# Second attention: three key blocks of a pass exponentiated on VectorE, value runs of two blocks, six sets of results

## What is computed

```python
q = (x @ wq + bq).reshape(B, Sq, H, D).transpose(0, 2, 1, 3)     # 16 heads of 8, Sq = 1024
k = (y @ wk + bk).reshape(B, -1, H, D).transpose(0, 2, 1, 3)     # 6404 keys
v = (y @ wv + bv).reshape(B, -1, H, D).transpose(0, 2, 1, 3)
scores = jnp.einsum('bhqd,bhkd->bhqk', q, k) / jnp.sqrt(D)
attn = jax.nn.softmax(scores, axis=-1)
out = jnp.einsum('bhqk,bhkd->bhqd', attn, v)
```

## Time and profile before

| what | value |
|---|---|
| median of 3 runs | 1854.99 us |
| profiled execution, its own time | 1853.31 us |
| its span, first to last instruction | 1851.5 us |
| mean granted TensorE clock | 0.924 of full speed |
| PE busy | 1582.9 us (85% of the span) |
| ACT busy | 1373.1 us (74%) |
| DVE busy | 854.8 us (46%) |
| POOL busy | 169.9 us (9%) |

### The profile page before, as it was taken

One profiled execution on the slowest core, in us unless ns is written; L12 is line 12 of the kernel. 1 busy time (PEld: TensorE's weight loads), 2 busy tenths in 40 slices (PEclk: granted clock), 3 DMA queues, 4 the chain that ended last, 5 costly groups with the idle time before them and its releaser, 6 DMA issues. The chain is left out here.

```text
span 1851.5 us, 22757 instructions
## 1 busy us (share of the span) xinstructions
PE 1582.9 (85%) x8261; PEld 603.4 (33%) x8261; DVE 854.8 (46%) x2331; ACT 1373.1 (74%) x1441; POOL 169.9 (9%) x154
## 2 busy tenths in 40 slices
PE   6789788898998993776789999999999999985996
PEld 4463354554554552533211111111111111113442
DVE  7768999999999997473400000000000000003223
ACT  5737687888887874313289999999999999982332
POOL 4840211111111101000000000000000000000000
PEclk8869899999999996787689999999999999997998
DMA  3430968979769679350000004000500000003000
GB/s 103 144 117 0 184 150 177 202 155 210 174 151 230 152 179 241 78 152 7 18 1 1 1 1 63 13 1 1 75 1 1 1 1 1 1 1 98 0 1 12
DMA packets 69263, 143.41 MB, mean 77 GB/s; under 512 B 21993, under 2 KB 40642, under 8 KB 68218
## 3 DMA queue, kind: packets, MB, share of 16 engines
q0 software_dynamic: 13616, 75.73, 20.5%
q1 hardware_dynamic: 55098, 65.30, 13.2%
q10 hardware_dynamic: 432, 0.85, 0.1%
HBM read 52.65 MB, written 13.99 MB: 36 GB/s over the span
## 5 line engine op out<-in xcount | busy, mean ns | idle before, releaser
L1936 ACT ACTIVATE ex<-ps 128x1536 f32<-128x1536 f32 x536 | 721.9, 1494 | 6.0 <-PE ps L1890 6.0
L1905 PE MATMUL ps<-ex,V 128*9 128x512 f32 x3200 | 419.8, 597 | 0.5 <-ACT ex L1936 0.4
L850 PE MATMUL ps<-K,qst 128*128 128x512 f32 (+1 forms) x832 | 392.9, 604 | 30.7 <-ACT srow L920 20.7
L1890 PE MATMUL ps<-Q,K 52*128 52x512 bf16 (+1 forms) x1632 | 322.8, 385 | 39.1 <-ACT ex L1936 34.2
L1946 DVE COPY o<-ps 9x512 f32<-9x512 f32 x32 | 22.0, 687 | 714.2 <-PE ps L1909 713.5
L1051 DVE MAX8 cand<-srow 128x8 f32<-128x200 f32 (+1 forms) x1024 | 318.7, 359 | 8.7 <-ACT srow L920 8.6
L1011 DVE SCALAR_TENSOR_TENSOR both<-srow,top,both 128x1536 f32<-128x1536 f32 (+1 forms) x128 | 239.4, 1870 | 21.2 <-ACT both L937 21.0
L920 ACT COPY srow<-ps 128x1024 f32<-128x1024 f32 (+1 forms) x224 | 205.1, 924 | 46.1 <-PE ps L850 45.7
L937 ACT ACTIVATE both<-srow,shift 128x1536 f32<-128x1536 f32 (+1 forms) x128 | 209.4, 1638 | 23.2 <-DMA both<-both 21.8
L1890 PEld LDWEIGHTS ps<-Q,K 52*128 52x128 bf16 (+1 forms) x1632 | 60.7, 94 | 448.1 <-ACT ex L1936 433.1
L850 PEld LDWEIGHTS ps<-K,qst 128*128 128x128 f32 x832 | 150.8, 198 | 166.5 <-issue 116.1
(11 more groups left out here) (333 smaller groups left out, 1087.2 us busy)
## 6 DMA issues: line engine op xcount, KB each, us to landing
both<-both POOLq DMA_DIRECT2D x69, 768.0 KB, 8.9
v_ring<-v_rows SPq DMA_DIRECT2D x84, 256.0 KB, 6.3
both<-both POOLq DMA_DIRECT2D x23, 898.0 KB, 13.1
K<-k_parts SPq DMA_DIRECT2D x48, 204.0 KB
k_parts<-kl SPq DMA_DIRECT2D x12, 384.0 KB, 2.6
V<-v_rows SPq DMA_DIRECT2D x4, 900.0 KB, 6.7
v_rows<-v1g SPq DMA_DIRECT2D x12, 288.0 KB, 3.8
srow<-v_rows SPq DMA_DIRECT2D x1, 3200.0 KB, 17.5
```

The source lines that it names most:

```text
L850: last = M.matmul(ps[:, BANK_OF[item] + b, 0:c1 - c0], qst[:, h, :], K0[:, c0:c1], start=True, stop=True)
L1890: last = M.matmul(out, K1[rows_, quad % 2, hh // 2, keys], Q1[rows_, 4 * quad + hh, tb * TB:(tb + 1) * TB], start=True, stop=True, tile_po ...
L1905: last = M.matmul(out, V1[:, quad % 2, g, VW * j:VW * j + VW], ex1[:, slot(w, 4 * g + j), :], start=g == 0, stop=False, tile_position=(0, ...
L1936: C.activation(ex1[:, s:s + NBANK, :], ps[:, b:b + NBANK, :], ACT.Exp)\
```

## The change

- **Scores in powers of two.** The queries' scale is multiplied by log2(e), and ScalarE's exponential takes scale = ln 2 and a bias. The bias is a tile of one value per partition, `common`, filled by POOL behind the clearing of `o1`; ScalarE waits for it once (`common_ready`).
- **Three key blocks per pass on VectorE.** Key blocks 47, 48 and 49 (12 tiles) no longer go through ScalarE. In units 6, 11, 16, ... 61 (`OWN`) ScalarE has only two tiles, and the third bank of the unit holds one of these 12 tiles. VectorE computes 2^x for it with nine dependent instructions of 512 elements (`power_of_two`): a maximum out of PSUM, an addition that rounds, six `scalar_tensor_tensor` and an integer shift. PE's scores wait for VectorE's reading of that bank too (`own_read`). ScalarE's part is 47 blocks and the last tile, 189 tiles, still in 67 units.
- **Values of two blocks in one run.** Key blocks 2i and 2i+1 are summed together behind the unit at which the second is ready. The values of VectorE's blocks follow behind units 26, 46 and 66 (`own_values`).
- **Six sets of results.** `ex1` has 18 slots (six units), `power` eight.

```diff
-        SC1 = float(DH1) ** -0.5
+        SC1 = float(DH1) ** -0.5 * LOG2E
...
-        NSLOT, NBANK = 12, 3
-        ex1 = sb(b8, "ex1", [P, NSLOT, TB])
+        NBANK, NHELD = 3, 6
+        BATCH, BATCHES, EVERY, FIRST_U = 4, 3, 5, 6
+        NOWN = BATCH * BATCHES
+        OWN = [FIRST_U + EVERY * i for i in range(NOWN)]
+        REGULAR = FULL1 - BATCHES
...
+        LATE_AT = {OWN[BATCH * (b + 1) - 1] + EVERY: b for b in range(BATCHES)}
+        LAST_OF = [min(4 * g + 3, NTILE - 1) for g in range(NSUM)]
+        READY_AT = [PLACE[tile][0] + 2 for tile in LAST_OF]
+        READY_AT = [READY_AT[min(g | 1, NSUM - 2)] if g < NSUM - 1 else READY_AT[g] for g in range(NSUM)]
...
                 PL.memset(o1[:, :, :], 0.0).then_inc(S("o1_zero"), 1)
+                PL.memset(common[:, :], float(np.log(1.0 / LEAD))).then_inc(S("common_ready"), 1)
...
                     if w * NU + u >= 2:
                         pe.wait_ge(S("exped1"), w * NU + u - 1)
+                        if own_before(w * NU + u - 1):
+                            pe.wait_ge(S("own_read"), own_before(w * NU + u - 1))
...
+                    if u in OWN:
+                        b, j = divmod(OWN.index(u), BATCH)
+                        last = score_tile(w, ps[:, bank(w, u, NBANK - 1), :], 0, REGULAR + b, j)
                     last.then_inc(S("scored1"), 1)
...
+                def own_values(w, b):
+
+                    quad = w // NB
+                    pe.wait_ge(S("powered"), w * NOWN + BATCH * (b + 1))
+                    for j in range(BATCH):
+                        last = M.matmul(ps[32 * j:32 * j + VW, 6 + w % 2, :], V1[:, quad % 2, REGULAR + b, VW * j:VW * j + VW],
+                                        power[:, (w * NOWN + BATCH * b + j) % (2 * BATCH), :], start=False, stop=False,
+                                        tile_position=(0, 32 * j))
+                    last.then_inc(S("power_used"), 1)
...
+                        if u in LATE_AT:
+                            own_values(w, LATE_AT[u])
...
+                act.wait_ge(S("common_ready"), 1)
...
-                        C.activation(ex1[:, s:s + NBANK, :], ps[:, b:b + NBANK, :], ACT.Exp)\
+                        C.activation(ex1[:, s:s + n, :], ps[:, b:b + n, :], ACT.Exp, scale=LN2, bias=common[:, 0:1])\
                             .then_inc(S("exped1"), 1)
...
+                def power_of_two(w, i):
+
+                    m = w * NOWN + i
+                    if m:
+                        dve.wait_ge(S("powered"), m)
+                    dve.wait_ge(S("scored1"), w * NU + OWN[i] + 1)
+                    V.tensor_scalar(score[:, :], ps[:, bank(w, OWN[i], NBANK - 1), :], LOW2, None, ALU.max)\
+                        .then_inc(S("own_read"), 1)
+                    dve.wait_ge(S("own_read"), m + 1)
+                    dchain(V.tensor_scalar(whole_[:, :], score[:, :], ROUND2, None, ALU.add))
+                    dchain(V.scalar_tensor_tensor(part[:, :], whole_[:, :], ROUND2, score[:, :], ALU.subtract, ALU.subtract))
+                    dchain(V.scalar_tensor_tensor(poly[:, :], part[:, :], POWER[4], part[:, :], ALU.add, ALU.mult))
+                    for k in (3, 2, 1):
+                        dchain(V.scalar_tensor_tensor(poly[:, :], poly[:, :], POWER[k], part[:, :], ALU.add, ALU.mult))
+                    bits = whole_[:, :].bitcast(I32)
+                    dchain(V.tensor_scalar(bits, bits, 23, None, ALU.logical_shift_left))
+                    if m // BATCH >= 2:
+                        dve.wait_ge(S("power_used"), m // BATCH - 1)
+                    V.scalar_tensor_tensor(power[:, m % (2 * BATCH), :], poly[:, :], POWER[0], whole_[:, :], ALU.add, ALU.mult)\
+                        .then_inc(S("powered"), 1)
```

More of the change, by code:

```diff
@@ L42 @@
 LOWEST = -3.0e38
-EXP_RANGE = 60.0
+LOG2E = float(np.log2(np.e))
+LN2 = float(np.log(2.0))
+EXP_RANGE = 60.0 * LOG2E
 LN_EPS = 1e-5
@@ L1853, in bank @@
[L1853 to L1857, removed]
+        NBANK, NHELD = 3, 6
[3 more added lines that the diff above has]
+        REGULAR = FULL1 - BATCHES
+        NPASS = NQ * NB
+        NTILE = 4 * REGULAR + 1
+        NSUM = REGULAR + 1
+        ex1 = sb(b8, "ex1", [P, NHELD * NBANK, TB])
+        power = sb(b8, "power", [P, 2 * BATCH, TB])
@@ new lines, in program @@
+        score, whole_, part = (sb(b8, name, [P, TB]) for name in ("score", "whole_part", "part"))
+        poly = score
+        common = sb(b8, "common", [P, 1])
+        UNITS, at = [], 0
+        while at < NTILE:
+            n = NBANK - 1 if len(UNITS) in OWN else NBANK
+            UNITS.append(list(range(at, at + n)))
+            at += n
+        NU = len(UNITS)
+        assert at == NTILE and max(OWN) + EVERY < NU
+        PLACE = {tile: (u, n) for u, tiles in enumerate(UNITS) for n, tile in enumerate(tiles)}
@@ L1859, in program, with block_of, own_before, bank @@
+        def block_of(g):
+            return g if g < REGULAR else FULL1
+        def own_before(k):
+            w, u = divmod(k, NU)
+            return w * NOWN + sum(1 for o in OWN if o < u)
+        def bank(w, u, n):
+            return (w * NU + u) % 2 * NBANK + n
+        def slot(w, u, n):
+            return (w * NU + u) % NHELD * NBANK + n
         with nc.Block() as block:
@@ L1873, in _, with score_tile @@
             def _(pe):
+                def score_tile(w, out, col, g, hh):
+                    quad, tb = divmod(w, NB)
+                    rows_ = slice(64 * (hh % 2), 64 * (hh % 2) + ROWS1)
+                    keys = slice(g * P, (g + 1) * P) if g < FULL1 else slice(g * P, g * P + LEFT)
+                    return M.matmul(out, K1[rows_, quad % 2, hh // 2, keys], Q1[rows_, 4 * quad + hh, tb * TB:(tb + 1) * TB],
+                                    start=True, stop=True, tile_position=(64 * (hh % 2), col))
                 def scores(w, u):
@@ L1879, in scores @@
                         pe.wait_ge(S("exped1"), w * NU + u - 1)
[L1880 to L1892, removed]
+                        if own_before(w * NU + u - 1):
+                            pe.wait_ge(S("own_read"), own_before(w * NU + u - 1))
+                    for n, tile in enumerate(UNITS[u]):
+                        g, j = block_of(tile // 4), tile % 4
+                        if g < FULL1:
+                            last = score_tile(w, ps[:, bank(w, u, n), :], 0, g, j)
+                        else:
+                            for hh in range(4):
+                                last = score_tile(w, ps[LEFT * hh:LEFT * (hh + 1), bank(w, u, n), :], LEFT * hh, g, hh)
+                    if u in OWN:
+                        b, j = divmod(OWN.index(u), BATCH)
+                        last = score_tile(w, ps[:, bank(w, u, NBANK - 1), :], 0, REGULAR + b, j)
                     last.then_inc(S("scored1"), 1)
@@ L1903, in values @@
                         out = ps[32 * j:32 * j + VW, 6 + w % 2, :]
-                        if g < FULL1:
-                            last = M.matmul(out, V1[:, quad % 2, g, VW * j:VW * j + VW], ex1[:, slot(w, 4 * g + j), :],
+                        if g < REGULAR:
+                            last = M.matmul(out, V1[:, quad % 2, g, VW * j:VW * j + VW], ex1[:, slot(w, *PLACE[4 * g + j]), :],
                                             start=g == 0, stop=False, tile_position=(0, 32 * j))
@@ L1908, in values @@
                             left = slice(LEFT * j, LEFT * (j + 1))
-                            last = M.matmul(out, V1[left, quad % 2, g, 0:VW], ex1[left, slot(w, NTILE - 1), :],
+                            last = M.matmul(out, V1[left, quad % 2, FULL1, 0:VW], ex1[left, slot(w, *PLACE[NTILE - 1]), :],
                                             start=False, stop=True, tile_position=(LEFT * j, 32 * j))
                     last.then_inc(S("summed1"), 1)
+                def own_values(w, b):
[6 more added lines that the diff above has]
+                    last.then_inc(S("power_used"), 1)
                 for w in range(NPASS):
@@ L1940, in _, with read_sums @@
             def _(dve):
-                dve.wait_ge(S("o1_zero"), 1)
-                for w in range(NPASS):
+                def read_sums(w):
                     quad, tb = divmod(w, NB)
-                    dve.wait_ge(S("summed1"), (w + 1) * NG)
+                    dve.wait_ge(S("power_used"), (w + 1) * BATCHES)
+                    dve.wait_ge(S("summed1"), (w + 1) * NSUM)
                     for j in range(4):
@@ L1947, in _ @@
                                       ps[32 * j:32 * j + VW, 6 + w % 2, :]).then_inc(S("o1_read"), 1)
+                def power_of_two(w, i):
[17 more added lines that the diff above has]
+                        .then_inc(S("powered"), 1)
+                dve.wait_ge(S("o1_zero"), 1)
+                for w in range(NPASS):
+                    if w:
+                        read_sums(w - 1)
+                    for i in range(NOWN):
+                        power_of_two(w, i)
+                read_sums(NPASS - 1)
     q1s.close()
```

38 lines of the change are left out of this document (16 added, 22 removed).

## The result

| | before | after |
|---|---|---|
| median of the runs shown with the result | 1856.63 us (4 runs) | 1948.51 us (4 runs) |
| ratio of the times, 95% interval | | 1.0506 [1.0484, 1.0528] |
| profiled execution, its own time | 1853.31 us | 1948.44 us |
| span | 1851.5 us | 1946.6 us |
| stage of the second attention, first to last exponential's start | 726.4 us (933.52 to 1659.96) | 814.6 us (940.26 to 1754.90) |

The change makes the kernel 5.1% slower; 1956 was forecast, in a range of 1928 to 1985.

What follows compares the result with a forecast made beforehand. ACT's own rate was taken to bound the kernel before; after the change, double runs with two score-bank sets. The profiled 1853.3 us plus 99 for the passes and 4 for the ends gave 1956 us, range 1928 to 1985.

Steps and rivals of the forecast that it cites:

- Part 3: Second attention, two blocks in one run: with two score-bank sets a pass takes 103.2 us against 90.76, +99 us in all.
- The parts of the cycle: Three units with a double run: scores to exponential 0.64, exponential 1.59, bank wait 0.06, run with scores 2.38; 4.67 us.
- The shorter cycles: Second attention: two-unit cycles take 2.87 us; three of the twenty three-unit cycles wait for a two-bank exponential, 0.43 shorter.
- ACT's busy time: Sign to look for in the second attention's profile after the change: ACT's busy time stays near 720 us.
- the pause in front of an exponential behind a run: Second attention: ACT idles 0.37 us before the exponential of the first scores; as a sign, some 0.4, 20-odd times a pass.
- part 2: Bias tile for ScalarE's exponentials in the second attention: 0.10 us more per instruction, in distance and duration, bounds 0 and 0.10.
- parts 1 and 4: Second attention: 12 shorter exponentials spare ACT 5.2 us a pass; VectorE takes 6.0 us a tile, keeps up, costs nothing.
- part 5: Ends of the second attention: +3 us at the start, waiting for `common` and the table load, +1 at the end.
- The clock: PE's granted clock with 1.3 us idle pieces: nothing counted; at 0.98, about 1.2 us a pass, 10 us in all.
- the second rival: VectorE becomes the bound: at 7.8 us a tile PE waits for `own_read`, +58 us, 2014 us; chance 0.06.
- The first rival: ACT remains the bound, the two bank sets absorbing double runs: 1856 or 1802 us; chances 0.06 faster, 0.03 the same.

Runs made afterwards that it cites:

- e2: The kernel before with runs of two blocks and 18 slots, nothing on VectorE, no pointer bias: 1924.53 us, ratio 1.0381, a pass 99.32 us.
- e1: The changed kernel with each block's values behind its own unit again (runs of one block): 1866.88 us, ratio 1.0065, a pass 92.06 us.
- e3: The changed kernel without the pointer bias, the common factor 2^10 sitting in VectorE's exponent bits: 1923.09 us, ratio 1.0373, a pass 99.55 us.
- e4: The changed kernel with runs of one block and no pointer bias: 1844.84 us, ratio 0.9940, a pass 89.43 us.
- e9: Three score-bank sets, runs of one, VectorE's blocks, no pointer, as e6, but VectorE's values behind units 42, 70, 97: 1824.17 us, ratio 0.9831, a pass 87.21.
- e7: The changed kernel with three more dependent instructions in each of VectorE's tiles: 2063.36 us in one execution, a pass 116.1 us.
- e8: The changed kernel with four sets of results held instead of six, runs of two kept: 2142.12 us in one execution, a pass 125.8 us.
- e5: Runs of two as in e2, no pointer, all blocks on ScalarE, but six score banks as three sets of two: 1871.67 us, ratio 1.0073, a pass 92.96.
- e6: e5 with runs of one block and VectorE's three blocks, every seventh unit from unit 10: 1834.72 us, ratio 0.9871, a pass 88.12 us.

## Why the prediction was right

**Which part decides.** Part 3 carried the forecast, and the two experiments that do it alone and undo it alone agree: + 8.6 (e2) and - 9.85 (e1) a pass. The parts of the cycle were forecast as 0.64 + 1.59 + 0.06 + 2.38 = 4.67; the trace has 2.37 for the run with its scores and 4.61 for the cycle. The shorter cycles came as forecast too: 2.86 for those of two units (forecast 2.87), 4.18 for those of three that wait for a two-bank exponential (forecast 4.24). The term that was off is the exponential: it lasts 1.54, not 1.59. I had added the 0.10 of the pointer to 1.49, the mean of the kernel before, where ACT runs without pause; where ACT pauses every few exponentials (e2, e3) they last 1.45, and the trace of before held one like that already, the last before the gap between two passes:

```profile
1027.12 1.46 ACT L1936 ACTIVATE ex<-ps 128x1536 f32<-128x1536 f32 x1
```

20 cycles x 0.05 are 1.0 of the 1.3 us by which the pass was forecast too long (103.2 against 101.9). That the total came within 7.5 us is in part luck: between the first and the last exponential the forecast is too high by 99 - 88.2 = 10.8 us, at the start and the end together by 1.5, and the earlier stages, longer by 4.5 in this execution for no reason that was forecast, take some of it back.

Two signs were wrongly stated. ACT's busy time was to stay near 720; the page has 747.2. The prediction's own cycle says as much: 103.2 less 24 pauses of 0.4 is 93.6 a pass, 749 in eight. And the pause in front of an exponential behind a run is not 0.37: by the prediction's own figures it is 0.64 - 0.43 = 0.21, and the records show 0.20. The 0.37 counts from where the next exponential could have started; it enters no sum.

**The pointer (part 2).** 0.10 was taken. In the changed kernel exponentials stand 1.42 to 1.44 apart where they follow at once, in e3 1.33 to 1.35, so it is 0.09, and they are 0.09 longer. With runs of two it costs 2.4 us a pass (e3), with runs of one 2.6 (e4 against e1), less than 67 x 0.09 = 6.0. In neither pair does ACT alone set the pace; that this is the reason was not tried apart. The Trainium skill ("ScalarE: Activation LUTs", What ACT_TABLE_LOAD costs) has about 93 ns for it; by that rule an exponential would last 1.45 + 0.09 = 1.54, which is what the trace shows.

**VectorE (parts 1 and 4).** Forecast were 6.0 us a tile and no wait for it; the trace has 1033.13 to 1039.10, 5.97, with an integer shift of 0.43 us like the other tensor_scalar out of SBUF, and no wait. What it saves ACT is worth nothing with runs of two (e3 against e2), 1.3 us a pass with runs of one (e4), and at least 4.0 with three sets: e9's 87.2 lies that far under the 201 x 0.427 + 101 x 0.053 = 91.2 that ACT alone would need there without it.

**The start (part 5).** Forecast +3:

```profile
936.68 3.51 POOL L1888 MEMSET o<- 128x4096 f32 x1 [65.53 <-POOLq L108]
...
937.82 1.28 ACT L1983 ACT_TABLE_LOAD   x1 [4.20 <-PE ps L1906]
940.13 0.09 POOL L1889 MEMSET common<- 128x1 f32 x1
940.26 5.83 ACT L1983 ACTIVATE ex<-ps,common 128x1536 f32<-128x1536 f32 x4 [1.16 <-POOL common L1889]
```

The table load no longer starts with the stage but 1.14 us later, and the exponential waits for `common`. From the stage's first instruction to the first exponential 3.58 us instead of 1.29: +2.3. The end cost 0.2 instead of 1.

**The clock.** Counted as nothing, and it stayed at 1.00. In e7, where PE idles for up to 2.9 us at a time, it was 0.95, and in e8, with idle pieces of up to 1.42, 0.92.

**Where the prediction was wrong.** "The six sets of results cost and give nothing" is false as a statement on what they are worth: nothing waits for them in the changed kernel, but with four sets it takes 2142 us (e8). I had looked only at what holds ACT while the six are there. The price of the second rival was too low: at 8.2 us a tile the pass is 116, where its formula gives 102 + 12 x 1.0 = 114, and it left out PE's wait for the fourth tile and the clock. The first rival, a run of two that is absorbed, does not hold with two sets of banks, and nearly holds with three (e5, 2.2 us a pass).

Left open: the division of the excess of e7 and e8, and the 4.5 us by which the earlier stages of the profiled execution were longer; among the kernels without a pointer the first exponential starts between 932.0 us (e9) and 941.1 (e4), so such differences come and go with the execution.

## What to carry to other kernels

Before work is gathered into longer runs on an engine that takes it in order, compare the run's length with what the consumer still has in its buffers when the run begins: here two sets, with 1.33 us of exponential in each, carried a run of one block (1.51 with its scores) and not one of two (2.37), though both engines had idle time. A trace often holds the case once, at a seam such as that between two passes; look for it there. Elements taken from an engine bring little if another sets the pace: 5.2 us of ScalarE's work were worth nothing with runs of two and 1.3 with runs of one. Where two engines pace each other, look at the depth of the buffer between them: the same six banks as three sets instead of two turned +8.6 us a pass into +2.2 for runs of two. For runs of one with VectorE's blocks, three sets and other places for VectorE's tiles turned -1.3 into -2.7 (e6), and VectorE's values moved apart into -3.6 (e9). Three sets with runs of one and nothing on VectorE were not run; by ACT's own rates (91.2 a pass, an estimate) they would not beat the kernel before.

## What the runs showed of the hardware that was not expected

- The same exponential (128 x 1536 out of PSUM) lasts 1.49 us in the mean in the kernel before, where ACT runs without pause, and 1.45 in e2 and e3, where it pauses every few exponentials. It is not a matter of what follows it: in e2 those with another at once behind them last 1.45, those with a pause behind them 1.46. The cause stays open. On the loop of this kernel the shorter one counted.
- A pointer bias costs 0.09 us of distance (1.33 to 1.42 between two that follow at once) and 0.09 of length (1.45 to 1.54) in each exponential (e3 against the changed kernel).
- PE's idle pieces of up to 1.4 us, every 4.6 us, left the granted clock at 1.00 with PE busy 79%; with idle pieces of 2.8 to 2.9 us up to three times a pass it was 0.95 over the stage (e7). The length of the single idle piece doesn't settle it: in e8 no piece from 950 us on is over 1.42 us, and the clock was 0.92.
- In a stretch at 1.2 GHz a run of two blocks lasted 3.35 us, at 2.4 GHz 1.91 (e8).
